# Feed-forward part of a decoder layer: tokens of experts 1 to 7 turned in 32 by 32 squares by VectorE and moved by sixteen transfers each, instead of turned by TensorE

## The reference, cut to what matters

```python
xn = (xf - mu) * jax.lax.rsqrt(var + EPS) * gamma + beta
tpe = T // E                                   # 128 tokens
xe = xn.reshape(MICRO_BATCHES, E, tpe, D)      # 4, 8, 128, 512
h = jax.nn.gelu(jnp.einsum('metd,edf->metf', xe, w1) + b1[None, :, None, :], approximate=False)
y = jnp.einsum('metf,efd->metd', h, w2) + b2[None, :, None, :]
out = xf + y.reshape(MICRO_BATCHES, T, D)
...
x = _layernorm(x + _L0_ffn_ref(x, ...), axis=-1)
```

## Time and profile before

| | |
|---|---|
| median of three runs | 1289.44 us (1288.36 to 1291.66) |
| profiled execution | 1288.53 us, of it span 1286.7 us |
| mean granted TensorE clock | 0.995 |
| PE busy, whole span | 1258.0 us (98%) |
| PE busy between 560 and 1260 us | 699.84 of 700.00 us |
| DVE, ACT, POOL busy, same stretch | 252.00, 275.64, 383.38 us |
| turning matmuls (L1537) of experts 1 to 7 | 112, in 28 groups of four |

### The profile page before, as it was taken

How to read it: one execution, slowest core, us unless ns; L and a number is a source line. 1 busy time by engine, 2 the same in 40 slices (tenths; PEclk the granted TensorE clock), 3 DMA queues, 4 the chain that set the end, 5 groups by cost and what they waited for, 6 DMA issues and landing times.

```text
span 1286.7 us, 19399 instructions
## 1 busy us (share of the span) xinstructions
PE 1258.0 (98%) x6794; PEld 1024.0 (80%) x6794; DVE 737.3 (57%) x1269; ACT 460.5 (36%) x629; POOL 743.4 (58%) x519
## 2 busy tenths in 40 slices
PE   8889999999999999899999999999999999999998
PEld 7678788888888888778888888888888888888886
DVE  5888888888888888953243343333423433433324
ACT  5223332333322232443534343434435335343330
POOL 4785666666666665657547365284384375464651
PEclk9989999999999999999999999999999999999999
DMA  8677877867777776537116125145063071061210
GB/s 276 151 142 155 161 155 149 157 157 158 155 154 154 154 156 118 160 111 253 66 41 229 66 99 190 48 149 187 2 227 108 1 269 66 33 237 66 96 68 33
DMA packets 161988, 172.33 MB, mean 134 GB/s; under 512 B 42940, under 2 KB 105356, under 8 KB 161932
## 3 DMA queue, kind: packets, MB, share of 16 engines
q1 hardware_dynamic: 161932, 171.55, 49.4%
HBM read 137.55 MB, written 17.18 MB: 120 GB/s over the span
## 4 chain that ended last, share of the span: by engine, by line
PE 56%; DVE 2%; issue 1%; DMA 0%; ACT 0%; POOLq 0%; POOL 0%; DVEq 0%
PE qk_ps L88 5%; PE qk_ps L87 5%; PE qk_ps L86 5%; PE gate_ps L86 5%; PE gate_ps L88 5%; PE gate_ps L87 5%; PE v_ps L86 5%; PE v_ps L88 5%; PE v_ps L87 4%; PE s_ps L86 2%; PE s_ps L88 2%; PE s_ps L87 2%; PE y_ps L86 2%; PE y_ps L88 2%; PE y_ps L87 2%; PE turn L1537 1%
## 5 line engine op out<-in xcount | busy, mean ns | idle before, releaser
L955 POOL TENSOR_TENSOR w_lo<-w_raw,w_hi 128x2048 fp32r<-128x2048 f32 x31 | 143.5, 4628 | 72.8 <-ACT w_hi L719 72.8
L947 POOL TENSOR_TENSOR w_lo<-w_raw,w_hi 128x2048 fp32r<-128x2048 f32 x32 | 148.0, 4624 | 10.6 <-ACT w_hi L729 10.6
L1037 DVE TENSOR_TENSOR_SCAN decays<-f_all,diag 128x384 f32<-128x384 f32 x128 | 153.0, 1235 | 0.6
L86 PE MATMUL qk_ps<-xT_parts,wqkv_hi 128*128 128x256 f32 x512 | 148.1, 289 | 1.4 <-DVE wqkv_lo L992 1.3
L1280 DVE CAST hid_hi<-gate_ps 128x512 fp32r<-128x512 f32 x62 | 42.9, 692 | 185.1 <-ACT gate_ps L753 178.8
L1280 DVE CAST hid_hi<-v_ps 128x512 fp32r<-128x512 f32 x62 | 42.9, 692 | 177.7 <-ACT v_ps L753 177.7
L88 PE MATMUL qk_ps<-xT_parts,wqkv_lo 128*128 128x256 f32 x512 | 144.3, 282 | 0.0
L87 PE MATMUL qk_ps<-xT_parts,wqkv_hi 128*128 128x256 f32 x512 | 144.2, 282 | 0.0
L919 POOL TENSOR_TENSOR rstd_b<-mean_var_b,ln_eps_b 128x4 f32<-128x4 f32 x15 | 3.0, 203 | 212.9 <-DVE mean_var_b L1265 211.3
L859 POOL TENSOR_TENSOR rot<-rot 128x256 f32<-128x256 f32 x64 | 64.0, 1001 | 78.5 <-DVE rot L1064 78.1
L753 ACT ACTIVATE gate_ps<-gate_ps,b_cols 128x512 f32<-128x512 f32 x64 | 42.2, 659 | 187.3 <-PE gate_ps L88 187.3
(11 more groups left out here) (229 smaller groups left out, 3156.0 us busy)
## 6 DMA issues: line engine op xcount, KB each, us to landing
w_raw<-in_w SPq DMA_DIRECT2D x64, 1024.0 KB, 7.5
f_all<-f_dram SPq DMA_DIRECT2D x16, 1024.0 KB, 4.8
qkT<-rot SPq DMA_DIRECT2D x256, 64.0 KB, 2.0
xT_raw<-in_xT SPq DMA_DIRECT2D x16, 512.0 KB, 12.5
x_both<-in_x SPq DMA_DIRECT2D x16, 512.0 KB, 11.4
f_all<-f_dram SPq DMA_DIRECT2D x16, 512.0 KB, 6.1
c_both<-in_ctx_in SPq DMA_DIRECT2D x16, 512.0 KB, 13.2
x_dram<-res SPq DMA_DIRECT2D x16, 512.0 KB, 13.9
```

What stands on the lines that cost most here:

```text
L86: eng.matmul(out, lhs_hi, rhs_hi, start=first, stop=False)
L947: pool.tensor_tensor(w2_lo[s % 2][:], w2_raw[s % 2][:], w2_hi[s % 2][:].bitcast(F32), ALU.subtract)\
L955: pool.tensor_tensor(w1_lo[s % 2][:], w1_raw[s % 2][:], w1_hi[s % 2][:].bitcast(F32), ALU.subtract)\
L1037: dve.tensor_tensor_scan(decays[:, n, :], f_all[:, n, :], diag[:], 0.0, ALU.mult, ALU.add).then_inc(decay_done, 1)
```

## The change

For the tokens of experts 1 to 7 TensorE's four groups of transposes and the waits around them are gone (expert 0, whose tokens are turned among the last attention batches, keeps them). Instead:

- VectorE's statistics come at c = 7 (were 8), ScalarE's scaling at c = 8 (was 9), right behind the rounding of slab 3 of w1 and ahead of that of w2.
- VectorE turns `xn` behind the split of chunk 9 (`turn_blocks`): four instructions of 128 x 512, one for each m, each of which transposes its sixteen 32 by 32 squares inside their 32 partitions, into a new tile `blocks`, which lies where the attention's `yT_hi` was.
- SP moves the squares to the partitions of their features (`move_tokens`): sixteen transfers, one for each pair of a source group and a target group of 32 partitions, each 32 partitions x 4 x 128 numbers, that is 64 KB in 128 runs of 512 bytes, from `blocks` back to `xn`. They stand between the loads of slab 4 and of slab 5 and wait for VectorE's four.
- ScalarE's `token_high` waits for all sixteen, reads `xn` in runs of 32 numbers, writes `blocks` (an SBUF tile, where it was a bank), and rounds that; VectorE takes the rest from `blocks`. This comes at c = 12 (k = 0), c = 13 (k = 1) and c = 14 (k = 2 and 3); it was one k at each of 11 to 14. At c = 12 and 13 it stands behind the rounding of the next expert's first slab.

```diff
+TOKENS_AT = {12: (0,), 13: (1,), 14: (2, 3)}
...
+            def move_tokens(e):
+
+                sp.wait_ge(blocks_done, (e - 1).after(NM, NM))
+                squares = blocks.rearrange("p k t -> p (k t)").rearrange("p (k g t) -> p k g t", g=GROUPS, t=P)
+                for g in range(GROUPS):
+                    for a in range(GROUPS):
+                        sp.dma_start(xn[g * SQUARE:(g + 1) * SQUARE, :, a * P:(a + 1) * P],
+                                     squares[a * SQUARE:(a + 1) * SQUARE, :, g, :]).then_inc(blocks_in, 16)
...
                     load_slab(e, 4)
+                    move_tokens(e + 1)
                     load_slab(e, 5)
...
+                    act.wait_ge(blocks_in, (e - 1).after(TURNED, TURNED))
+                    turned = xn[:, k, :].rearrange("p (a m j) -> p m a j", a=GROUPS, m=NM)
+                    into = bank.rearrange("p (m a j) -> p m a j", a=GROUPS, m=NM)
...
-                    if c == 9 and more:
+                    if c == 8 and more:
                         expert_normalize(e + 1, 0)
-                    if more and 11 <= c < 11 + KC:
-                        token_high(e + 1, c - 11)
+                    for k in TOKENS_AT.get(c, ()) if more else ():
+                        token_high(e + 1, k)
...
+            def turn_blocks(e):
+
+                if e.i is not None or e.n >= 2:
+                    dve.wait_ge(blocks_in, (e - 2).after(TURNED, TURNED))
+                into = blocks.rearrange("p k t -> p (k t)").rearrange("p (b m j) -> p b m j", m=NM, j=SQUARE)
+                for m in range(NM):
+                    dve.wait_ge(xn_done, e.after(NM, m + 1))
+                    dve.transpose(into[:, :, m, :], xn[:, m, :].rearrange("p (b j) -> p b j", j=SQUARE)).then_inc(blocks_done, 1)
...
-                        if c == 8:
+                        if c == 7:
                             expert_stats(e + 1, 0)
-                        if 11 <= c < 11 + KC:
-                            token_low(e + 1, c - 11)
+                        if c == 9:
+                            turn_blocks(e + 1)
+                        for k in TOKENS_AT.get(c, ()):
+                            token_low(e + 1, k)
...
-                    if more and 11 <= c < 11 + KC:
-                        turn_tokens(e + 1, c - 11)
```

More of the change, by code:

```diff
@@ L292, in layer_program @@
     xnT_lo = [later("xnT_lo0", home["wqkv_lo"]), later("xnT_lo1", home["qkT"])]
+    blocks = later("blocks", home["yT_hi"], T, KC, F32)
     x2b = c_both[:]
@@ L308, in layer_program @@
     minus_one = sb("minus_one", [P, NM])
+    SQUARE = 32
+    GROUPS = P // SQUARE
+    TURNED = 16 * GROUPS * GROUPS
     def token_bank(e, k):
+        if not by_bank(e):
+            return blocks[:, k, :]
         if e.i is None and e.n == 0 and k >= 2:
@@ L314, in token_bank, with by_bank @@
         return turn[k % 2]
+    def by_bank(e):
+        return e.i is None and e.n == 0
     acc = [y_ps, s_ps, qk_ps[:, 0:D], qk_ps[:, D:2 * D]]
@@ L330, in layer_program @@
     e_minus_mean, e_shift_done = [sem(f"minus_mean_b{n}") for n in range(2)], [sem(f"shift_done_b{n}") for n in range(2)]
+    blocks_done, blocks_in = sem("blocks_done"), sem("blocks_in")
     xn_done, xn_turned, xnT_done = sem("xn_done"), sem("xn_turned"), sem("xnT_done")
@@ L731, in token_high @@
             def token_high(e, k):
-                act.wait_ge(xn_turned, e.after(KC, k + 1))
-                bank = token_bank(e, k)
-                act.activation(bank[:], bank[:], ACT.Identity, bias=beta_sb[:, k:k + 1],
+                bank = token_bank(e, k)[:]
+                if by_bank(e):
+                    act.wait_ge(xn_turned, KC * e.n + k + 1)
+                    turned, into = bank, bank
+                else:
+                    act.wait_ge(blocks_in, (e - 1).after(TURNED, TURNED))
+                    turned = xn[:, k, :].rearrange("p (a m j) -> p m a j", a=GROUPS, m=NM)
+                    into = bank.rearrange("p (m a j) -> p m a j", a=GROUPS, m=NM)
+                act.activation(into, turned, ACT.Identity, bias=beta_sb[:, k:k + 1],
                                scale=gamma_sb[:, k:k + 1]).then_inc(xnT_done, 1)
                 act.wait_ge(xnT_done, e.after(KC, k + 1))
-                act.activation(xnT_hi[e.odd][:, k, :], bank[:], ACT.Copy).then_inc(xnT_hi_done, 1)
+                act.activation(xnT_hi[e.odd][:, k, :], bank, ACT.Copy).then_inc(xnT_hi_done, 1)
             def expert_normalize(e, n):
@@ L742, in expert_normalize @@
                 act.wait_ge(e_shift_done[n], e.after(1, 1))
-                if n == 0 and e.n >= 1:
-                    act.wait_ge(xn_turned, e.after(KC, 0))
-                elif n == 0:
+                if n == 0 and e.n == 1 and e.i is None:
+                    act.wait_ge(xn_turned, KC)
+                elif n == 0 and by_bank(e):
                     act.wait_ge(qk_mm, NB * (B - 1))
@@ L1527, in turn_tokens @@
                     pe.wait_ge(xn_done, e.after(NM, NM))
-                if e.n >= 1 or e.i is not None:
-                    pe.wait_ge(xnT_lo_done, e.after(KC, k - 1))
-                elif k < 2:
+                if k < 2:
                     pe.wait_ge(probs_done, NH * (B - 1))
```

## The result

| | before | after |
|---|---|---|
| median | 1289.38 us (1288.36 to 1291.66, four runs) | 1276.78 us (1275.80 to 1278.20, four runs) |
| ratio | | 0.9906 (0.9893 to 0.9918) |
| profiled execution | 1288.53 us, span 1286.7 | 1276.49 us, span 1274.5 |

The change makes the kernel faster by 0.9%. The forecast was 1277.0 us, with a range of 1273.5 to 1282.0.

What follows compares the result with a forecast made beforehand. TensorE, never idle in the experts, was taken as the bound. Removing 28 transpose groups saves 12.4 us, the new path costs nothing: 1288.53 less 12.4 is 1276.1, plus 0.9 for the median, 1277.0 us; range 1273.5 to 1282.

Steps and rivals of the forecast that it cites:

- The bound: TensorE, 560 to 1260 us: busy 699.84 of 700.00 us, so only its own work or new waits count.
- The price of what was removed: TensorE's 28 groups of four transposes: 0.442 us each by distance of starts, 12.4 us in all, 1.77 an expert.
- The transposes by VectorE: Four at c = 9, taken as 0.69 us each, ending at 795.2; at 1.65 each, 799.0; nothing lost either way.
- The transfers: SP's sixteen moves behind VectorE's transposes: 10.8 us to issue, 2.6 to land, last landing at 808.6; worst 816.8.
- the rival that counted runs (1313): Sixteen moves paced by 2048 runs: 21.6 us, landing 819.4, 5.1 us late, 36 us in all; slower (1294 to 1313) 0.06.
- Its place: ScalarE at c = 12, waiting for the sixteenth landing with GELU 13 behind it; TensorE feels it at down(13).
- The limit: Moves may land as late as 814.3 before TensorE waits at down(13), 5.7 us behind the forecast landing.
- ScalarE at c = 12: Tokens wanted once rounding ends by 809.5; moves landed at 808.6 make nobody wait, by 0.9 us.
- counted as no cost: ScalarE reading SBUF in runs of 32 where it was a bank: even doubled, 1.5 us each, c = 14 holds 4.2 us.
- one us for each us of wait: Landings beyond 814.3: each us costs one in each of seven experts; from 816.1 on slower than before.
- The slower rival: Moves come too late at ScalarE, c = 12, and TensorE waits at down(13): 1294 to 1313 us, chance 0.06.
- The own range of the matmuls' step: Step may hang on where instructions lie; all slow loses 8.1 us, about 1285; own range 1274.5 to 1280; 1280 to 1285: 0.09.

Runs made afterwards that it cites:

- turns_back: Changed kernel with four unused identity transposes put back on TensorE at the end of steps 11 to 14, experts 0 to 6: 1288.41 us, ratio 1.000 to the kernel before.
- behind: Changed kernel with the sixteen moves queued behind the loads of slab 5 instead of ahead of them: 1277.39 us, ratio 0.9902 to the kernel before.
- halves: Changed kernel with each of the sixteen moves issued as two, 32 transfers of 32 KB: 1309.51 us, ratio 1.0157 to the kernel before.
- bank: Changed kernel with ScalarE writing scaled tokens into the two banks TensorE's transposes used, instead of SBUF: 1276.70 us, ratio 0.9902 to the kernel before.

## Why the prediction was right

*The bound* was read from the stage itself, and it held: TensorE had no waits to give back, and got none.

*The price of what was removed.* 28 groups at 0.442 us, 12.4 us, from the distance of starts. `turns_back` lies 11.6 us above the changed kernel's median, with about 1 us of doubt in each, and its own 28 groups cost 0.442 us each again; the kernel before lies 12.6 above it, and the spans differ by 12.2. The length of one transpose in the trace, 272 ns, would have given 30 us. The Trainium skill's page "VectorE: DVE Perf Modes" says under "Rules for kernel authors" that TensorE is to turn where PSUM will do as the target; on this engine, which is busy all the time, that was the slower way. The 390 ns that its section "The three transpose paths" gives for a bfloat16 turn by TensorE are not what one costs in these runs, 0.110 us in float32.

*The transposes by VectorE.* Taken as 0.69 us, that of an ordinary pass; 0.670 measured. Four take 2.48 us on the timeline.

*The transfers.* From the attention's moves: 10.8 us for sixteen and 2.6 to land. Measured 10.28 and 2.1. They overlap. The Trainium skill gives a fixed 2.0 us in "DMA: Bandwidth & Descriptors", "Anatomy of one DMA"; that section is on transfers that GpSimd issues, which the prediction doesn't say, while SP issues these. The 2.1 us to landing are close to its figure all the same, the 5.4 in `behind` are not. The pace comes from the issue, 0.60 us a transfer whatever its runs: the rival that counted runs (1313) is refuted by the 32 moves. Its place was right, though: once the moves are late, TensorE stops at `down(13)`. The limit was right too. It had the moves land at the latest 3.5 us ahead of `down(13)`; in `halves` TensorE waits, in all seven experts, by just so much as ScalarE, which starts on them when they land, starts later than 3.6 us ahead of it.

*ScalarE at c = 12* had 0.9 us of room by my sum and has 2.2 (landed near 804.1, wanted at 806.28): transposes, issues and landing each took a little less. A wait of 2.3 us there costs TensorE nothing (`behind`).

*What was missed, without effect on the time.* First, `xnT_lo` with both operands in SBUF, which I had counted as no cost because the scalings read and write SBUF at the pace of a bank. That row was of ScalarE; the edit also changed VectorE's operands, and those I did not price. It has VectorE stand for 44 us in all (14 passes, 3.2 us more each) and took 1.4 us of the room ahead of `down(13)` (3.2 us in `bank`, 1.8 here) and as much ahead of `down(14)`. It doesn't move the limit of 814.3, since GpSimd's pass is over by the time such late tokens reach VectorE; but it adds a second place to stop at, `down(14)`, that the prediction did not have: 1.3 us in two experts of `halves`. Second, the price of a late move: I had one us for each us of wait, and it is up to 2.7 us more for each wait, for the clock. The slower rival was priced too low for its wait.

*The own range of the matmuls' step* (to 1285 if all went slow) had a wrong reason: code that is moved doesn't move the pattern. The pattern did change, beside the removed groups, but its mean over the 247 chunks went only from 0.2303 to 0.2301 us. It did no harm, but it was doubt without ground.

## What to carry to other kernels

On an engine that is never idle, price an instruction by the distance of its neighbours' starts with and without it, not by its length, and check the gain by putting dummies back. A detour through slower engines is free as long as its last landing leaves room at the first instruction that the full engine waits for; work that room out by name (here `down(13)`), and leave some over, since a wait past it can cost more than itself. When a tile moves from a bank to SBUF, look at every reader's operands and at what GpSimd does at that time.

## What the runs showed of the hardware

- VectorE's pass with two SBUF operands stands still while GpSimd's pass with two SBUF operands runs: 3.85 us against 0.69, or 1.05 to 1.77 where it starts late, always ended 0.55 us behind GpSimd's end. VectorE's transposes with one SBUF operand ran beside the same GpSimd pass at full pace (2.48 us for four, below), and so did passes with one operand in a bank.
- VectorE transposes the sixteen 32 by 32 squares of 128 x 512 float32 numbers in 0.67 us, no more than an ordinary pass.
- A 64 KB or 32 KB transfer between partitions of SBUF costs 0.60 us of the issuing queue either way, and lands 2 us later (median 2.1 and 1.9), or 5.4 where sixteen stood right behind two loads of 1 MB.
- A wait of 2.4 to 3.6 us on a TensorE that had been busy all the time was followed in eleven of fourteen cases by 7 to 13 matmuls at half clock, 1.4 to 2.7 us more; in three, of 2.5 to 3.2 us, by none. What decides between the two stays open.
- The mean step of a chunk's matmuls varied between 0.227 and 0.233 us at full granted clock (1.00) in a pattern that was the same in kernels with the same TensorE sequence (`turns_back` and the kernel before), whatever the other engines did.

The rows for the second half of the first point, the timelines of VectorE and GpSimd in the kernel after:

```profile
789.23 2.48 DVE L1303 STREAM_TRANSPOSE blocks<-xn 128x512 f32<-128x512 f32 x4
```

```profile
789.77 4.64 POOL L976 TENSOR_TENSOR w_lo<-w_raw,w_hi 128x2048 fp32r<-128x2048 f32 x1 [0.83 <-ACT w_hi L752]
```
